# Eight-core TTT layer with a mixture of experts: zeroing the experts' row blocks from GpSimd in pieces, and loading the experts' rows plainly with a transpose on TensorE

## The reference

```python
x = L0_attn_in_seq                                   # 4 x 4096 x 1024
mod = (_silu(L0_c) @ L0_wmod).reshape(L0_c.shape[0], 6, 1, -1)
h = _layernorm(x) * (1 + ca) + sa
# per token, in order: pred = W k + b; g = 2/d (pred - v); W -= LR g k^T; b -= LR g; out = W q + b
x = x + ga * _L0_attn_ref(h, theta_K, theta_V, theta_Q, W0, b0)
h = _layernorm(x) * (1 + cb) + sb
scores = softmax(h @ router_w); topk_scores, topk_idx = top_k(scores, 2)      # 8 experts
y_e = (silu(h @ gate_w[e]) * (h @ up_w[e])) @ down_w[e]                       # F = 1024
shared = silu(h @ shared_gate_w) * (h @ shared_up_w) @ shared_down_w          # F = 2048
x = x + gb * (shared + sum over the two chosen experts of score * y_e)
```

## Time and profile before

| | |
|---|---|
| time, three runs | 1726.4, 1728.81, 1732.52 us; median 1728.81 |
| the profiled execution: its time, and the span of its slowest core | 1728.16 us; 1726.6 us (core 1) |
| spans of the odd cores (role 1) | 1726.6, 1723.3, 1714.3, 1700.5 us |
| spans of the even cores (role 0) | 1658.8, 1656.5, 1671.6, 1653.4 us |
| core 1: TensorE busy | 1411.2 us, 82% of the span |
| core 1: VectorE, ScalarE, GpSimd busy | 735.8, 461.3, 300.5 us |

### The profile page before, as it was taken

The page is one execution under the profiler, slowest core; times in us unless marked ns, Lnnn a source line. Parts: engine busy times, 40 slices in busy tenths (PEclk is TensorE's granted clock), DMA queues, the critical chain, the costliest instruction groups (busy, mean ns, idle before and its releaser), DMA issues.

```text
span 1726.6 us, 22112 instructions; the slowest of 8 cores (1653.4 to 1726.6 us)
## 1 busy us (share of the span) xinstructions
PE 1411.2 (82%) x7569; PEld 691.7 (40%) x7569; DVE 735.8 (43%) x1278; ACT 461.3 (27%) x752; POOL 300.5 (17%) x207
## 2 busy tenths in 40 slices
PE   0377988672699999999997899998495894989897
PEld 0333443331345444445444444543142341434354
DVE  1526363730546455585466424532021121222576
ACT  1144353331445444454343321010010110101010
POOL 0038787500131000000010110000000000000221
PEclk9989999895899999999998999999698997999999
DMA  7963438349902012231264559579989999892863
GB/s 181 254 122 114 107 114 277 61 71 189 276 13 74 13 37 78 76 95 47 86 124 121 158 115 206 165 180 167 185 144 164 192 160 210 146 198 86 320 205 122
DMA packets 121859, 244.13 MB, mean 141 GB/s; under 512 B 40197, under 2 KB 40325, under 8 KB 120710
## 3 DMA queue, kind: packets, MB, share of 16 engines
q0 software_dynamic: 46384, 108.55, 32.9%
q1 hardware_dynamic: 60950, 104.63, 21.3%
q10 hardware_dynamic: 14400, 29.36, 6.9%
HBM read 254.07 MB, written 78.64 MB: 193 GB/s over the span
## 4 chain that ended last, share of the span: by engine, by line
PE 67%; DMA 10%; DVE 8%; issue 5%; another core or an unknown queue 4%; ACTq 3%; ACT 1%; POOL 1%; SPq 0%; DVEq 0%; POOLq 0%
PE prep L617 9%; PE gate L850 6%; PE up L850 6%; PE u L870 6%; PE prep L870 5%; PE u L779 4%; PE up L847 4%; PE gate L847 4%; DMA xb<-x 4%; PE up L709 3%; ACTq L935 3%; PE up L682 3%; DMA w1u<-suw 3%; PE gate L682 3%
## 5 line engine op out<-in xcount | busy, mean ns | idle before, releaser
L1303 DVE TENSOR_TENSOR act<-up,sgb 128x512 bf16<-128x512 f32 (+1 forms) x128 | 84.1, 657 | 380.3 <-PE up L850 256.7
L1014 ACT ACTIVATE sgb<-gate 128x512 bf16<-128x512 f32 (+1 forms) x128 | 73.0, 571 | 608.6 <-PE gate L850 370.6
L1184 DVE TENSOR_TENSOR WT<-WT,u 128x512 f32<-128x512 f32 x240 | 153.4, 679 | 44.8 <-PE u L779 44.6
L779 PE MATMUL u<-Gsb,Ktk 128*128 128x512 bf16 x480 | 128.2, 391 | 45.2 <-DVE WT L1184 44.2
L984 ACT CAST Wbf<-WT 128x1024 bf16<-128x1024 f32 x120 | 124.7, 1040 | 70.6 <-issue 55.1
L617 PE MATMUL prep<-hft,s_thK 128*128 128x512 bf16 x512 | 124.8, 393 | 8.5 <-DVE s_thK L1095 3.8
L850 PE MATMUL gate<-hfe,pair 128*128 128x512 bf16 x256 | 65.3, 401 | 78.2 <-DMA hfe<-hx 78.2
L699 PE MATMUL gate<-Wbf,Kft 128*128 128x512 bf16 x256 | 82.7, 399 | 48.6 <-ACT Wbf L984 48.6
L1483 POOL DMA_INDIRECT hx<-h2m,sl x28 | 29.2, 1045 | 420.8 <-DVE sl L1286 415.1
L779 PEld LDWEIGHTS u<-Gsb,Ktk 128*128 128x128 bf16 x480 | 43.8, 99 | 102.4 <-issue 66.6
L1429 POOL TENSOR_SCALAR x2b<-x2b,silc 128x1024 f32<-128x1024 f32 x28 | 80.7, 2881 | 13.4 <-DMA x2b<-wmod 12.3
(11 more groups left out here) (239 smaller groups left out, 2305.8 us busy)
## 6 DMA issues: line engine op xcount, KB each, us to landing
hx<-zero ACTq DMA_DIRECT2D x2, 10240.0 KB, 83.2
xb<-x SPq DMA_DIRECT2D x32, 512.0 KB
x2b<-wmod POOLq DMA_DIRECT2D x32, 512.0 KB, 5.5
yx<-ring SPq DMA_DIRECT2D x32, 512.0 KB, 5.4
wmb<-wmod SPq DMA_DIRECT2D x8, 1024.0 KB, 7.8
hx<-zero ACTq DMA_DIRECT2D x2, 4096.0 KB, 28.7
pair<-gw POOLq DMA_DIRECT2D x4, 2048.0 KB, 34.0
w1u<-uw POOLq DMA_DIRECT2D x4, 2048.0 KB, 46.5
```

The source lines that it names most:

```text
L779: m = t.matmul(U[jh][:, 0:512], Ktk[s % 2][:, cc * D + dt * P:cc * D + (dt + 1) * P], Gsb[:, cc * D + jh * 512:cc * D + (jh + 1) * 512], s ...
L1184: v.tensor_add(w, w, U[jh][:, 0:512]).then_inc(S["v_W"], 1)
L1303: v.tensor_mul(act[k % 2][:, fj * ACW:fj * ACW + COLS[k]], R[2 + n % 2][:, 0:COLS[k]], sgb[n % 2][:, 0:COLS[k]]).then_inc(v_act, 1)
```

## The change

The zeroing moves from ACT to GpSimd. Where ACT issued it in the middle of the first stage, with rows of one row block over the 128 partitions, GpSimd now issues it after it has stored `gbs`: one DMA for all row blocks below `CAP`, and four for the slots beyond (role 1: all four at once behind the first; role 0: one after the scatters of each of its first four supersteps). Each of the four has its own semaphore, and the scatter that could first use its slots waits for it. All descriptors now read the same row of `d_zero`.

The experts' rows are loaded by ACT with a plain DMA into one buffer `hxb` (tokens on the partitions). TensorE transposes them in groups of eight 128x128 blocks into one PSUM bank (`bkT`), between the half-rows of `down(k)` for expert block `k + 2`, and ACT copies each group into the one remaining `hfe`. ACT issues the load of expert `e + 1` when the last transposes of expert `e` are done. The PSUM bank comes from `Y`, which has three banks in place of four.

```diff
-        if NPRE and s == 2:
-            fill[5] += [("zero", 0)]
-        if s == (4 if NPRE else 0):
-            fill[6] += [("zero", 1)]
...
-        Y = (U[0], U[1], A[0], A[1])
+        bkT = At[1]
+        Y = (U[0], U[1], A[0])
...
-                hfe = [ectx.enter_context(nc.sbuf_tensor(f"hfe{i}", [P, DT * ACW], BF16)) for i in range(2)]
+                hfe = ectx.enter_context(nc.sbuf_tensor("hfe", [P, DT * ACW], BF16))
+                hxb = ectx.enter_context(nc.sbuf_tensor("hxb", [P, ACW // P * D], BF16))
...
                     if kind == "e":
-                        t.wait_ge(ld_hx[i % 2], 16 * (i // 2 + 1))
+                        t.wait_ge(a_xT, TEW * (i + 1))
...
+                def expert_rows(e, r):
+                    if r == 0:
+                        t.wait_ge(ld_hx, 16 * (e + 1))
+                    if e or r:
+                        t.wait_ge(a_xT, TEW * e + r)
+                    for i in range(DT):
+                        m = t.transpose(bkT[:, i * P:(i + 1) * P], hxb[:, r * D + i * P:r * D + (i + 1) * P],
+                                        s_ident[:, :])
+                    m.then_inc(p_xT, 1)
...
-                        if q >= 4:
-                            t.wait_ge(v_y, q - 3)
+                        if q >= 3:
+                            t.wait_ge(v_y, q - 2)
...
+                        if k + 2 < NB and BLK[k + 2][0] == "e":
+                            for r in range(TEW):
+                                if r * HALVES[k] // (TEW + 1) == h:
+                                    expert_rows(BLK[k + 2][1], r)
...
-                        lo, n = ((0, CAP * NE // P), (CAP * NE // P, (REG - CAP) * NE // P))[arg[0]]
-                        for i in range(2):
-                            s_.dma_start(ap(d_hx, (lo + i * n // 2) * P * D, [[D, P], [P * D, n // 2], [1, D]]),
-                                         ap(d_zero, 0, [[D, P], [0, n // 2], [1, D]])).then_inc(hx_zeroed[arg[0]], 16)
...
+                def load_rows(e):
+                    if e == 0:
...
+                    else:
+                        s_.wait_ge(p_xT, TEW * e)
+                    s_.dma_start(ap(hxb, 0, [[ACW // P * D, P], [D, TEW], [1, D]]),
+                                 ap(d_hx, e * CAP * D, [[D, P], [P * D, TEW], [1, D]])).then_inc(ld_hx, 16)
...
+                    if k + 1 < NB and BLK[k + 1][0] == "e":
+                        e = BLK[k + 1][1]
+                        for r in range(TEW):
+                            s_.wait_ge(p_xT, TEW * e + r + 1)
+                            s_.copy(ap(hfe, r * P, [[DT * ACW, P], [CAP, DT], [1, P]]),
+                                    ap(bkT, 0, [[1024, P], [P, DT], [1, P]])).then_inc(a_xT, 1)
+                        if e + 1 < NE:
+                            load_rows(e + 1)
...
+                def zero_rows(lo, step, n, done):
+                    g.dma_start(ap(d_hx, lo * D, [[D, n], [step * D, NE], [1, D]]),
+                                ap(d_zero, 0, [[0, n], [0, NE], [1, D]])).then_inc(done, 16)
...
+                zero_rows(0, CAP, CAP, hx_zeroed)
+                if NPRE:
+                    for j in range(4):
+                        zero_beyond(j)
...
-                    sy.dma_start_transpose(ap(hfe[e % 2], 0, [[DT * ACW, P], [CAP, DT], [1, CAP]]),
-                                           ap(d_hx, e * CAP * D, [[D, CAP], [1, D]])).then_inc(ld_hx[e % 2], 16)
```

More of the change, by code:

```diff
@@ L85, in build_schedule @@
         out += [("row", 2, i) for i in range(4)]
-        out += [("bc", row, jh) for row in (4, 5) for jh in range(2)] + [("xe",), ("zero", 0)]
+        out += [("bc", row, jh) for row in (4, 5) for jh in range(2)] + [("xe",)]
     for s in range(NS):
@@ L304, in build_program @@
         ld_row = [sem("ld_row0"), sem("ld_row1")]
-        hx_zeroed = [sem("hx_zeroed0"), sem("hx_zeroed1")]
+        hx_zeroed, beyond_zeroed = sem("hx_zeroed"), [sem(f"beyond_zeroed{j}") for j in range(4)]
         ld_w0, ld_thK, ld_thV, ld_thQ, ld_rw = (sem(n) for n in ("ld_w0", "ld_thK", "ld_thV", "ld_thQ", "ld_rw"))
@@ L321, in build_program @@
         st_out = sem("st_out")
-        p_g2, p_u2, p_y = (sem("p_" + n) for n in ("gate", "up", "y"))
-        a_own, a_c, a_init, a_W0, a_g2 = (sem("a_" + n) for n in ("own", "c", "init", "W0", "gate"))
+        p_xT, p_g2, p_u2, p_y = (sem("p_" + n) for n in ("xT", "gate", "up", "y"))
+        a_own, a_c, a_init, a_W0, a_xT, a_g2 = (sem("a_" + n) for n in ("own", "c", "init", "W0", "xT", "gate"))
         v_own, v_mod, v_flag, v_act, v_y, v_x3, v_z, v_out = (sem("v_" + n) for n in (
@@ L849, in gate_up @@
                         elif CAP <= 512:
-                            m = t.matmul(banks[n % 2][:, 0:CAP], q, hfe[i % 2][:, ht * CAP:(ht + 1) * CAP],
+                            m = t.matmul(banks[n % 2][:, 0:CAP], q, hfe[:, ht * CAP:(ht + 1) * CAP],
                                          start=(ht == 0), stop=(ht == DT - 1))
@@ L854, in gate_up @@
                                 o = ht * CAP + half * HC
-                                m = t.matmul(banks[half][:, 0:HC], q, hfe[i % 2][:, o:o + HC],
+                                m = t.matmul(banks[half][:, 0:HC], q, hfe[:, o:o + HC],
                                              start=(ht == 0), stop=(ht == DT - 1))
@@ L889, in beyond @@
                                     m = t.matmul(b[:, 0:rows], w[:, ht * D + fj * P:ht * D + (fj + 1) * P],
-                                                 hfe[0][:, ht * CAP:ht * CAP + rows], start=(ht == 0), stop=(ht == DT - 1))
+                                                 hfe[:, ht * CAP:ht * CAP + rows], start=(ht == 0), stop=(ht == DT - 1))
                                 m.then_inc(done, 1)
@@ L930, in scalar_prog @@
                                 ap(At[BANK[step, 0]], 0, [[1024, P], [P, DT], [1, P]])).then_inc(S["a_x"], 1)
-                    elif kind == "zero":
-                        lo, n = ((0, CAP * NE // P), (CAP * NE // P, (REG - CAP) * NE // P))[arg[0]]
-                        for i in range(2):
-                            s_.dma_start(ap(d_hx, (lo + i * n // 2) * P * D, [[D, P], [P * D, n // 2], [1, D]]),
-                                         ap(d_zero, 0, [[D, P], [0, n // 2], [1, D]])).then_inc(hx_zeroed[arg[0]], 16)
                     elif kind == "vrow":
@@ L1029, in beyond @@
                             s_.activation(sgb[0][:, 0:rows], R[0][:, 0:rows], AF.Silu).then_inc(o_sg, 1)
-                s_.wait_ge(v_flag, 1)
+                def load_rows(e):
+                    if e == 0:
+                        s_.wait_ge(st_hx[0], 16 * NCH)
+                        s_.wait_ge(st_hx[1], 16 * NCH)
+                        s_.wait_ge(v_flag, 1)
+                        for i in range(2):
+                            s_.wait_ge(st_x2[i], 16 * NCH // 2)
+                            s_.wait_ge(st_h2[i], 16 * (NCH - 4) // 2)
+                    else:
+                        s_.wait_ge(p_xT, TEW * e)
+                    s_.dma_start(ap(hxb, 0, [[ACW // P * D, P], [D, TEW], [1, D]]),
+                                 ap(d_hx, e * CAP * D, [[D, P], [P * D, TEW], [1, D]])).then_inc(ld_hx, 16)
+                load_rows(0)
                 s_.reg_load(flag_reg, flag[0:1, 0:1])
@@ L1476, in gpsimd_prog @@
                     if step[1] == NPRE // 2:
-                        g.wait_ge(hx_zeroed[0], 32)
-                    if step[1] == NPRE // 2 + CAP // (2 * P):
-                        g.wait_ge(hx_zeroed[1], 32)
+                        g.wait_ge(hx_zeroed, 16)
+                    for j in range(4):
+                        if step[1] == NPRE // 2 + (CAP + OVC * j) // (2 * P):
+                            g.wait_ge(beyond_zeroed[j], 16)
                     for c16 in (2 * step[1] - NPRE, 2 * step[1] - NPRE + 1):
@@ L1486, in gpsimd_prog @@
                                 h2m[:, (c16 % 2) * D:(c16 % 2 + 1) * D], None).then_inc(st_hx[c16 % 2], 16)
+                    if not NPRE and step[1] < 4:
+                        zero_beyond(step[1])
                 g.wait_ge(v_flag, 1)
@@ L1621, in sync_moe @@
                     load_x2(n)
-                for e in range(2):
-                    load_rows(e)
                 for n in range(NCH):
@@ L1646, in beyond @@
                             sy.wait_ge(o_u, DT * x)
-                        sy.dma_start_transpose(ap(hfe[0], 0, [[DT * ACW, P], [CAP, DT], [1, rows]]),
+                        sy.dma_start_transpose(ap(hfe, 0, [[DT * ACW, P], [CAP, DT], [1, rows]]),
                                                ap(d_hx, row0 * D, [[D, rows], [1, D]])).then_inc(o_hx, 16)
```

12 lines of the change are left out of this document (5 added, 7 removed).

## The result

The changed kernel takes 1892.7 us (median of 4 runs, 1879.5 to 1922.5) against 1730.1 for the kernel before: 1.091 times, with a 95% interval of 1.086 to 1.096. It is 9% slower; I had forecast 5% faster. All eight cores lost. (Medians are of all runs; ratios, and spans of cores, leave out runs in which a die ran at a lower clock.) The fence has the span and granted clock of the cores that the earlier trace rows show.

A forecast was written before the change was run, and what follows sets the result against it. Odd cores end last, held by TensorE's waits for experts' rows and for ACT, stuck issuing zeroing. 1728.2 - 47 (zeroing moved) - 46 (experts' rows) + 2 = 1637, on the median 1638 us; range 1608 to 1692.

The forecast's parts named there:

- The two stalls: TensorE in core 1: 78.2 us waiting for transposed experts' rows, 48.6 us for ACT's cast, held by issuing the second zeroing DMA.
- Part 2: Experts' rows in odd cores, plain load and TensorE transposes for the transposing DMA: gain 46 us (19 to 67), 2 us charged.
- The cadence: Time per expert from expert 2 on in odd cores: 47 us, bound by weight loads; bounds 44.5 and 51.
- Part 1: Zeroing leaves ACT in odd cores: 67 us saved less 20 us for moved traffic, gain 47 us (27 to 67).
- all 29.4 MB at that rate last 143 us: Odd cores' zeroing stream from GpSimd: keeps the 206 GB/s of the old large DMAs, done before the first scatter at 174 us.
- rival E: Slower than before: one-row zeroing stream is slow, scatters queue behind it; some 1880 us at a third rate; chance below 95 GB/s 0.05.
- the traffic term: Cost of the moved zeroing traffic to odd cores' loads of x: 20 us, bounds 0 to 40.
- 20 us for 143 us of stream: Traffic price in odd cores, scaled from 13.6 us lost in about 99 near the old large zeroing.
- C: Plain load of experts' rows lands late beside the weights, in 50 us not 40: + 52 us, 1690; chance 0.06.
- D: Plain load of experts' rows as slow as the transpose, Part 2 worth 0 or less: 1681 to 1696 us; chance 0.04.
- B: Even cores set the time if weights keep up: about 1628 us, or 1653 if traffic hurts them twice as much; chance 0.15.

The follow-up runs named there:

- src_rows: Changed kernel, but each zeroing DMA reads a distinct row of d_zero per group of eight rows, not one row for all: 1665.5 us, 0.962 of before.
- rows_only: Changed kernel with the zeroing of before put back on ACT, only the experts' rows loaded in the new way: 1696.2 us, 0.981 of before.
- bench1: Separate program of eight 8.4 MB zeroing DMAs, differing in source, destination order and issuer: one source row 87 to 98 us, 8 rows or more 51 to 55.

## Why the prediction was wrong

**What bounds the kernel, and both gains: right.** The two stalls were on the path and went. Mark 6 came 71.8 us earlier (forecast 66.9); src_rows gives 69.2.

**Part 2: right in the place I read, too high for the whole.** The cadence was forecast at 47 us and was 47.2, the wait for weights took over from that for rows, copies cost nothing to be seen, the plain load landed in 16 us. Mark 14 to the end gained 46.8 us in core 1 (51 in rows_only), forecast 44. But alone Part 2 was worth 33: the sum had no term for what rows_only loses ahead of mark 14, 13 us in core 1, of which 7 are ACT's longer hold and 6 have no known cause. The forecast read core 1 of one execution; over 25 runs of the kernel before the four odd cores' mean spans are 1712 to 1715 us, so none of them is the slow one as a rule. One term was also 3 us short: by the earlier trace rows the weights land 51.8 us after the first issue, not 49. The Trainium skill's rule that transposing DMAs are as fast as plain ones (Advanced Engine Details and Errata, X-Bar Transpose (TRN2)) does not hold for this kernel: in core 1 the median transpose took 49 us from issue to landing, the median plain load of the same block 16, and the rule would have made Part 2 worth nothing.

**Part 1: the step that failed** is "all 29.4 MB at that rate last 143 us", at 206 GB/s. The rate came from rows in which 128 different rows were read, and was used for DMAs that all read one. It was 67 GB/s and 440 us. I had seen the difference, wrote it down as rival E, gave it 0.05 for being slower than 95 GB/s, and left it out of the bounds of the traffic term, 0 to 40 us; the true cost of that term was 267. E had the mechanism (the stream slow, the scatters behind it) and its price at a third of the rate, some 1880 us, against 1893. That it came so near is in part luck. Its inner split was off: it has 200 us for the scatters' wait and 60 for traffic (the sum's 20 and 40 more), and measured were 118 and 149, because the loads of x held the supersteps back so that the scatters came later. The chance had no row behind it in either direction, and should have been weighed as an unknown with a large price: no row showed this access pattern, and one DMA alone would have shown it.

**The second step that failed** is the size of the traffic even at a healthy rate, 20 us for 143 us of stream; it was 40 for 161 (src_rows, marks 6 to 10). I had divided the 13.6 us lost near the large zeroing by its 99 us. But 47 of these were ACT's hold, and in them TensorE and DVE, stalled anyway, could lose next to nothing. The stretch in the kernel before (its length, then busy us of PE, PEld, DVE, ACT and POOL, granted clock, DMA share, GB/s):

```profile
371.00:418.00 47.00, 5.52 (x26) 2.30 (x24) 0.86 (x2) 0.00 (x0) 0.00 (x0) 0.60 0.89 162
```

Over the remaining 52 it is 0.26 us per us, which gives 42 for 161. That this fits so well is in part luck: by the table above a us of stream cost 0.15 to 0.47 us, depending on the source and the amount. Some 7 of the 40 come from the even cores' pieces, as far as the kernels with the source in SBUF tell.

**The others.** C and D did not happen: the plain load is fast, and no transpose waited for it. B did not either, though the slowest even core of src_rows ends at 1624 to 1639, near the 1628 forecast. The Trainium skill's statement that issuers share the same 16 DMA engines (DMA: Bandwidth & Descriptors, Issuing engines are not separate DMA queues) agrees with bench1 in that the same transfer took 51.3 us from SP and 55.1 from GpSimd. It told me that moving the issue is harmless, which the runs bear out, and I let it cover the access pattern, which had changed in the same line.

## What to carry to other kernels

A DMA source with step 0 over everything, from DRAM, makes all descriptors read one row: alone it ran at 58 to 97 GB/s where distinct rows gave 160, and SBUF as a source 312. Give each partition its own row of the constant, or keep it in SBUF; two rows far apart do not help, and four only in part. When a change moves a transfer and rewrites its access pattern, no rate from the old trace holds for it, and a price that nothing bounds belongs into the range. A cost measured beside a stall is too low, since the stalled engines could lose nothing then; divide by the time in which they could.
